# Graph kernel on one core: bias splits padded to 128 rows, one stacked matmul for four, and the end of a graph's preparation two units earlier

## What is computed

```python
# layer 0
adj0 = adj + eye; dis = adj0.sum(2) ** -0.5
x = layernorm(x + dis[:, :, None] * adj0 * dis[:, None, :] @ (x @ weight) + bias)
# layer 1
m_j = x @ W1[:D];  m_i = x @ W1[D:]
pre = m_j[:, None, :, :] + m_i[:, :, None, :] + b1          # one row per pair (i, j)
msg = gelu(layernorm(pre) * g1 + be1)
agg = einsum('bijo,bij->bio', msg, adj)                     # adj is about 6% full
out = layernorm(x + layernorm(concat([x, agg]) @ W2 + b2) * g2 + be2)
```

## Time and profile before

| | us |
|---|---|
| median of 3 runs | 4361.47 (4359.83 to 4365.68) |
| profiled execution | 4369.12 |
| its span | 4367.4 |
| PE busy, matmul | 4004.6 (92%) |
| ACT busy | 3479.5 (80%) |
| DVE busy | 3154.2 (72%) |
| POOL busy | 1499.9 (34%) |

### The profile page before, as it was taken

One profiled execution on the slowest core, in us unless ns is written; L12 is line 12 of the kernel. 1 busy time (PEld: TensorE's weight loads), 2 busy tenths in 40 slices (PEclk: granted clock), 3 DMA queues, 4 the chain that ended last, 5 costly groups with the idle time before them and its releaser, 6 DMA issues.

```text
span 4367.4 us, 95715 instructions
## 1 busy us (share of the span) xinstructions
PE 4004.6 (92%) x30270; PEld 3283.8 (75%) x30399; DVE 3154.2 (72%) x6981; ACT 3479.5 (80%) x9481; POOL 1499.9 (34%) x1205
## 2 busy tenths in 40 slices
PE   3799999999989999999999999999999999999998
PEld 2677777777768777778777777777777777777776
DVE  3577777777767777767777768777777777768776
ACT  2687888878868878877887878888888888878887
POOL 2333432233413334323343233343233343223331
PEclk8899999999989999999999999999999999999999
DMA  1222221122202222112221112222122221112210
GB/s 42 72 70 78 70 73 38 57 79 78 71 24 64 79 70 78 44 52 72 78 71 65 41 61 78 79 70 68 37 62 79 78 71 62 46 59 78 66 58 15
DMA packets 245645, 276.71 MB, mean 63 GB/s; under 512 B 22320, under 2 KB 204080, under 8 KB 245040
## 3 DMA queue, kind: packets, MB, share of 16 engines
q1 hardware_dynamic: 212272, 168.62, 12.9%
q0 software_dynamic: 32768, 100.70, 6.2%
HBM read 160.17 MB, written 109.05 MB: 62 GB/s over the span
## 4 chain that ended last, share of the span: by engine, by line
PE 56%; ACT 12%; issue 11%; POOL 9%; DVE 5%; DMA 4%; SPq 2%; POOLq 0%; DVEq 0%; ACTq 0%; PEldq 0%
PE z_even_ps L1264 11%; POOL table L449 9%; PE agg_odd_ps L1227 9%; PE z_odd_ps L1264 8%; PE agg_even_ps L1227 7%; ACT tmp L647 4%; PE z_even_ps L1260 3%; PE z_odd_ps L1260 2%; DMA nbr_heavy<-table 2%; PE p_ps L1146 2%; PE p_ps L1147 2%; PE p_ps L1090 2%; DMA table<-stage,row_id 2%; ACT msg L634 2%; ACT root L578 1%
## 5 line engine op out<-in xcount | busy, mean ns | idle before, releaser
L647 ACT ACTIVATE tmp<-nbr,r_sb 128x128 f32<-128x128 f32 x4864 | 1519.3, 389 | 29.1
L998 DVE SCALAR_TENSOR_TENSOR pick<-rank,root_p 128x512 f32<-128x512 bf16 (+3 forms) x1664 | 895.5, 566 | 69.8 <-ACT rank L597 69.8
L1028 DVE SCALAR_TENSOR_TENSOR spread<-rankT,nbr 128x512 f32<-128x512 bf16 (+3 forms) x1664 | 918.7, 580 | 0.0
L449 POOL DMA_INDIRECT table<-stage,row_id x512 | 617.9, 1207 | 551.5 <-issue 504.9
L1264 PEld LDWEIGHTS z_even_ps<-mi_g,pick 128*128 128x128 f32 x5120 | 643.9, 201 | 152.2 <-issue 152.2
L634 ACT ACTIVATE msg<-msg 128x768 f32<-128x768 f32 (+1 forms) x896 | 727.7, 812 | 32.3 <-issue 29.2
L1264 PE MATMUL z_even_ps<-mi_g,pick 128*128 128x129 f32 x5120 | 733.0, 295 | 0.0
L1264 PEld LDWEIGHTS z_odd_ps<-mi_g,pick 128*128 128x128 f32 x5120 | 608.8, 192 | 144.8 <-issue 144.8
L1264 PE MATMUL z_odd_ps<-mi_g,pick 128*128 128x129 f32 x5120 | 694.9, 285 | 0.0
L1227 PE MATMUL agg_odd_ps<-spread,msg 128*128 128x128 f32 x5120 | 671.8, 282 | 21.4 <-DVE spread L1028 19.3
L1227 PEld LDWEIGHTS agg_odd_ps<-spread,msg 128*128 128x128 f32 x5120 | 636.0, 199 | 24.1 <-DVE spread L1028 23.5
(11 more groups left out here) (206 smaller groups left out, 5129.6 us busy)
## 6 DMA issues: line engine op xcount, KB each, us to landing
nbr<-table SPq DMA_DIRECT2D x128, 512.0 KB, 4.0
adj_g<-in_adj SPq DMA_DIRECT2D x32, 1024.0 KB, 5.5
nbr_root<-table SPq DMA_DIRECT2D x128, 256.0 KB, 4.7
nbr_heavy<-table SPq DMA_DIRECT2D x512, 32.0 KB, 3.6
x_g<-in_x SPq DMA_DIRECT2D x32, 256.0 KB, 2.9
table<-stage,row_id POOLq DMA_INDIRECT x512, 2.7
out<-out_sb SPq DMA_DIRECT2D x32, 256.0 KB, 2.3
w_sb<-in_L_gnn_W SPq DMA_DIRECT2D x2, 128.0 KB, 2.3
```

Of the source, the lines that this page charges most:

```text
L449: pool.indirect_dma_start(table[q], bass.IndirectOffsetOnAxis(ap=row_id[:, jt * TB + it:jt * TB + it + 1], axis=0), stage[:, jt, it, :], N ...
L647: last = act.activation(tmp[:, c % 2, n - FROM[u], :], half_row, ACT.Identity, scale=r_sb[:, c % 2, n - FROM[u]:n - FROM[u] + 1])
L998: ins = dve.scalar_tensor_tensor(into.rearrange("p k n -> p (k n)"), rank[:, it, span], float(MARK + t), root_p[:, it, span], ALU.is_equal ...
L1028: ins = dve.scalar_tensor_tensor(into, rankT[:, it, jt:jt + count, :], float(MARK + t), nbr[:, it, jt:jt + count, 0:P], ALU.is_equal, ALU. ...
```

## The change

1. `be_split`, `mi_split` and `b2_split` have 128 partitions, zero from row 3 on, and the 3-row matrix of ones is replaced by the 128 x 128 one that exists already. The results are the same.
2. `T_HEAVY` is one matmul with 128 columns of weights in place of four with 32; for it DVE copies `edge_p[:, 0:32]` four times side by side (`edge_heavy`).
3. The norms go to four spare columns (400 to 403) of the bank `agg_odd_ps` with semaphores of their own, so they no longer take a place in the line for `p_ps` and stand in one step with the first `S_V`.
4. `S_Y`'s pair, `S_H`, `S_HT`, `S_MIT`, `S_MJT` and `S_NRM` stand one unit earlier, `S_V`, `S_MJ`, `S_MI`, `S_SEED`, `S_ROOT`, `S_OVER` and `S_SCATTER` two (the last read of `S_OVERS` one).

```diff
-S_Y, S_H, S_HT, S_MIT, S_MJT, S_NRM = 9, 12, 13, 14, 15, 16
-S_V = (17, 18, 19, 20)
-S_HB, S_MJ, S_MI, S_SEED, S_ROOT, S_SCATTER, S_OVER, S_OVERS = 18, 21, 22, 21, 23, 24, 23, 27
+S_Y, S_H, S_HT, S_MIT, S_MJT, S_NRM = 9, 11, 12, 13, 14, 15
+S_V = (15, 16, 17, 18)
+S_HB, S_MJ, S_MI, S_SEED, S_ROOT, S_SCATTER, S_OVER, S_OVERS = 18, 19, 20, 19, 21, 22, 21, 26
...
+NORM = 400
...
-        be_split = sb("be_split", [3, 3, D + 1], BF16)
-        ones3 = sb("ones3", [3, P], BF16)
+        be_split = sb("be_split", [P, 3, D + 1], BF16)
...
-                if s == S_Y + 1:
+                if s == S_Y:
                     wait_alone(pool, y_seq, a * POWS + 1)
...
                 if s == S_NRM:
-                    filled(F_NRM)
-                    act.activation(norm_j[:, :], p[:, 0:TB], ACT.Identity, scale=1.0 / D).then_inc(p_ev, 1)
-                    act.wait_ge(p_ev, a * NF + (F_NRM + 1))
+                    act.wait_ge(p_norm, a + 1)
+                    act.activation(norm_j[:, :], agg_ps[1][:, 0, NORM:NORM + TB], ACT.Identity, scale=1.0 / D).then_inc(p_normed, 1)
+                    act.wait_ge(p_normed, a + 1)
...
-                if (s, slot) == (S_Y + 2, 2):
+                if (s, slot) == (S_Y + 1, 2):
...
-                if (s, slot) == (S_PLACE, 0):
+                if (s, slot) == (S_POS, 4):
                     dve.wait_ge(p_fill, a * NF + (F_POS + 1))
...
+                if (t, slot) == (T_EDGE + 1, 2):
+                    dve.wait_ge(t_ev, n * NR + (R_EDGE + 1))
+                    dve.tensor_copy(edge_heavy[:, :, :], edge_p[:, 0:HEAVY_W].unsqueeze(1).to_broadcast([P, HEAVY_T, HEAVY_W])).then_inc(t_edge, 1)
...
                 if s == S_NRM:
-                    free(F_NRM)
+                    pe.wait_ge(p_ev, a * NF + (F_MJT + 1))
+                    if not is_int(a, 1):
+                        pe.wait_ge(p_normed, a)
                     for jt in range(TB):
-                        last = mm(p[:, jt:jt + 1], sqj[:, jt * P:(jt + 1) * P], ones[:, 0:1], start=True, stop=True)
-                    last.then_inc(p_fill, 1)
+                        last = mm(agg_ps[1][:, 0, NORM + jt:NORM + jt + 1], sqj[:, jt * P:(jt + 1) * P], ones[:, 0:1], start=True, stop=True)
+                    last.then_inc(p_norm, 1)
...
-                    for m in range(HEAVY_T):
-                        last = mm(p[m * HEAVY_W:(m + 1) * HEAVY_W, 0:P], edge_p[:, 0:HEAVY_W], lower[:, :], start=True, stop=True)
-                    last.then_inc(t_fill, 1)
+                    pe.wait_ge(t_edge, n + 1)
+                    mm(p[:, 0:P], edge_heavy[:, :, :].rearrange("p k w -> p (k w)"), lower[:, :], start=True, stop=True).then_inc(t_fill, 1)
...
-                        mm(z[:, h, :, :].rearrange("p k w -> p (k w)"), ones3[:, :], be_split[:, :, :].rearrange("p k w -> p (k w)"),
+                        mm(z[:, h, :, :].rearrange("p k w -> p (k w)"), ones_b[:, :], be_split[:, :, :].rearrange("p k w -> p (k w)"),
```

More of the change, by code:

```diff
@@ L55 @@
 S_X, S_SUP, S_PROD, S_PRE, S_CNT, S_CLS, S_POS, S_PLACE = 3, 5, 6, 8, 9, 10, 11, 12
-S_Y, S_H, S_HT, S_MIT, S_MJT, S_NRM = 9, 12, 13, 14, 15, 16
-S_V = (17, 18, 19, 20)
-S_HB, S_MJ, S_MI, S_SEED, S_ROOT, S_SCATTER, S_OVER, S_OVERS = 18, 21, 22, 21, 23, 24, 23, 27
[L60 to L63, removed]
+S_Y, S_H, S_HT, S_MIT, S_MJT, S_NRM = 9, 11, 12, 13, 14, 15
+S_V = (15, 16, 17, 18)
+S_HB, S_MJ, S_MI, S_SEED, S_ROOT, S_SCATTER, S_OVER, S_OVERS = 18, 19, 20, 19, 21, 22, 21, 26
+F_XT, F_AT, F_SUP, F_PROD, F_CNT, F_POS, F_HT, F_MIT, F_MJT, F_MJ, F_MI = (
+    0, 1, 5, 6, 7, 8, 9, 10, 11, 16, 17)
+F_V = (12, 13, 14, 15)
+F_OVER, NF = 18, 19
+NORM = 400
 SORT_FROM = 3
@@ L106, in adj_resnorm_kernel @@
         rest = sb("rest", [P, D])
-        b2_split = sb("b2_split", [3, D], BF16)
-        mi_split = sb("mi_split", [3, D], BF16)
-        be_split = sb("be_split", [3, 3, D + 1], BF16)
-        ones3 = sb("ones3", [3, P], BF16)
+        b2_split = sb("b2_split", [P, D], BF16)
+        mi_split = sb("mi_split", [P, D], BF16)
+        be_split = sb("be_split", [P, 3, D + 1], BF16)
         classes = sb("classes", [P, CLASSES])
@@ L171, in adj_resnorm_kernel @@
         edge_p = sb("edge_p", [P, N], BF16)
+        edge_heavy = sb("edge_heavy", [P, HEAVY_T, HEAVY_W], BF16)
         rank = sb("rank", [P, TB, N], BF16)
@@ L219, in adj_resnorm_kernel @@
         p_scat = [sem(f"p_scat{jt}") for jt in range(TB)]
-        p_seed, p_sq, p_new, p_cube, p_left = (sem(f"p_{n}") for n in ("seed", "sq", "new", "cube", "left"))
+        p_norm, p_normed, p_seed, p_sq, p_new, p_cube, p_left = (sem(f"p_{n}") for n in ("norm", "normed", "seed", "sq", "new", "cube", "left"))
         x_seq, y_seq, z_seq = sem("x_seq"), sem("y_seq"), sem("z_seq")
@@ L223, in adj_resnorm_kernel @@
         t_root = [sem(f"t_root{k}") for k in range(2)]
-        t_fill, t_ev, t_heavy, t_over = (sem(f"t_{n}") for n in ("fill", "ev", "heavy", "over"))
+        t_fill, t_ev, t_edge, t_heavy, t_over = (sem(f"t_{n}") for n in ("fill", "ev", "edge", "heavy", "over"))
         (c_pick, c_spread, c_zp, c_r, c_tmp, c_z, c_msg, c_agg) = (
@@ L723, in _ @@
             step(dve.tensor_tensor(b1_all, b1_all, g1_all, ALU.mult))
-            split(mi_split[:, :], b1_all)
-            split(b2_split[:, :], b2_all)
-            step(dve.memset(be_split[:, :, :], 0.0))
+            for rows in (mi_split[:, :], b2_split[:, :], be_split[:, :, :]):
+                step(dve.memset(rows, 0.0))
+            split(mi_split[0:3, :], b1_all)
+            split(b2_split[0:3, :], b2_all)
             for k in range(3):
-                split(be_split[:, k, 0:D], be1_all)
-            step(dve.memset(ones3[:, :], 1.0))
+                split(be_split[0:3, k, 0:D], be1_all)
             step(dve.memset(x_v[:, :], 1.0))
@@ L1129, in prepare @@
                         if s == S_MI:
-                            last = mm(dst, ones3[:, :], mi_split[:, :], start=False, stop=True)
+                            last = mm(dst, ones_b[:, :], mi_split[:, :], start=False, stop=True)
                     last.then_inc(p_fill, 1)
                 if s == S_NRM:
-                    free(F_NRM)
+                    pe.wait_ge(p_ev, a * NF + (F_MJT + 1))
+                    if not is_int(a, 1):
+                        pe.wait_ge(p_normed, a)
                     for jt in range(TB):
-                        last = mm(p[:, jt:jt + 1], sqj[:, jt * P:(jt + 1) * P], ones[:, 0:1], start=True, stop=True)
-                    last.then_inc(p_fill, 1)
+                        last = mm(agg_ps[1][:, 0, NORM + jt:NORM + jt + 1], sqj[:, jt * P:(jt + 1) * P], ones[:, 0:1], start=True, stop=True)
+                    last.then_inc(p_norm, 1)
                 if s == S_OVER:
@@ L1197, in overflow @@
                                 pe.wait_ge(o_sp, n + 1)
-                            mm(cols[:, :, 0:D + 1], ones3[:, :], be_split[:, 0:2, :], start=True, stop=False, skip_group_check=True)
+                            mm(cols[:, :, 0:D + 1], ones_b[:, :], be_split[:, 0:2, :], start=True, stop=False, skip_group_check=True)
                             for jt in (2 * k, 2 * k + 1):
@@ L1242, in steps @@
                     mm(u, aggT[:, k % 2, :], w2_sb[:, 1, :], start=False, stop=False)
-                    mm(u, ones3[:, :], b2_split[:, :], start=False, stop=True).then_inc(e_u, 1)
+                    mm(u, ones_b[:, :], b2_split[:, :], start=False, stop=True).then_inc(e_u, 1)
                 a, s = cx.prepared(i)
```

## The result

| | median us | lowest to highest | runs |
|---|---|---|---|
| kernel before | 4363.58 | 4359.83 to 4370.76 | 4 |
| changed kernel | 4059.80 | 4031.62 to 4082.12 | 4 |

The ratio is 0.9299 (95% interval 0.9239 to 0.9358): 304 us less, where 323 less was forecast, and 4059.8 where 4040 was. The profiled execution of the changed kernel took 4082.12 us with a span of 4080.3; against the 4369.12 of before that is 287 less. Its granted clock is 0.974 over the span.

The account below looks back on a forecast made before the run. ACT limits stage A (units 11 to 22), PE the other 16 units, stage B. 149 + 17 + 16 + 8 + 98 + 78 - 43 = 323 us less gives 4040 us, range 3930 to 4165.

Parts of the forecast that it names:

- padding in B: Bias groups of z in the 16 units limited by PE: 128 rows save 0.30 us a unit, 149 us.
- `b2_split`: Its bias groups for 2.3 tiles in the PE-limited stage: 128 rows save 0.24 us each, 17 us.
- A's yield: Units 11 to 22, limited by ACT: PE's savings mostly hidden, 0.5 us a graph counted, 16 us.
- the wait: PE's wait for tile 0's rows at L1159: transfers leave two units earlier, so it goes, 98 us.
- the low clock: Clock drop behind PE's wait at L1159: goes with the wait, 2.5 us a graph, 78 us.
- DVE's backlog: Unit of the wait at L1159: DVE work the wait hid costs back 1.4 us a graph, -43 us.
- a padded group keeps its cost: Rival at the bias groups: weight loads cannot run under matmuls of the same row group; 4214 us, chance 3%.
- A yields too: Rival in the ACT-limited stage: PE's 12 x 0.30 us count there, 112 us more, 3928 us; chance 11%.
- The low clock did not stay: Rival: the low clock stays or finds another place, as PE idles at ACT's root; 4118 us, chance 12%.
- ACT did not take B over: Rival in the PE-limited stage: ACT or DVE becomes its limit, gains there lost; 4214 us, chance 8%.
- Late all the same: Rival at tile 0's read: something else than the last indirect transfer holds SP; 133 us less gain, 4173, chance 3%.
- The slower outcome: Rival: PE idles behind the root in every graph and the clock stays at 1.2 GHz; 4702 us, chance 3%.

Follow-up runs that it names:

- 64-row kernel: The changed kernel with only the bias group ahead of z cut from 128 to 64 rows: 4204.7 us, ratio 0.9627 to the kernel before.
- semaphore kernel: The changed kernel with a semaphore for the 13th transfer, so SP's tile 0 read skips waiting for transfers 14 to 16: 4017.7 us, changed kernel 4078.9.
- 64- and 65-row kernels: The changed kernel with only the bias group ahead of z at 64 or 65 rows: 4204.7 us with 64, 4089.2 with 65.

## Right and wrong, point by point

The forecast of 323 us stands against 287 between the two profiled executions (and 304 between the medians):

| term | predicted | measured | from |
|---|---|---|---|
| padding in B | 149 | 149 | 0.30 us a unit, by starts and by the 64-row kernel |
| `b2_split` | 17 | 17 | units with it 0.54 shorter |
| A's yield | 16 | 0 | 50.85 to 50.90 |
| T_HEAVY | 8 | 8 | by starts, 0.16 to 0.056; not run alone |
| the wait | 98 | 41 | 97.7 to 56.4 |
| the low clock | 78 | 70 | 293.6 to 154.2 us at 1.2 GHz, half of the difference |
| DVE's backlog | -43 | about 0 | the rest |

The measured terms sum to 285 of 287. Part 1 and parts 3 and 4 were never run apart without the gaps above, so the split between them rests on the starts, the waits and the clock records, and for z's padding on the 64-row kernel.

That the total came so near is partly luck. For the wait, its clock and the backlog the prediction had 98 + 78 - 43 = 133, for a wait that goes; 41 + 70 = 111 came with half of the wait still there. With the wait gone, in the semaphore kernel, the same terms against the kernel before are 88 for the wait (97.7 to 10.0) and 108 for the clock (293.6 to 78 us at 1.2 GHz, half of the difference), less the 14 above: 182. With the 174 of the padding and T_HEAVY that is 356, and the spans differ by 355 (4367.4 and 4012.1). So the prediction was wrong that the wait goes and priced its going too low, and the two errors cancel in part.

- **Padding: right.** The way in, the group and the way out each lost what the rows of before said, 0.10 us. The rival by which a padded group keeps its cost (4214) falls. The Trainium skill's rule in TensorE: Matmul & The Clock Gate (What overlaps and what doesn't), that a load runs under a matmul only where the row group differs, is not borne out: z's first load stopped standing idle just when its rows became the same. The Trainium skill's TensorEngine Tiling (Key Properties) has a change of mode drain the engine; the 64- and 65-row kernels agree, with 0.10 in and 0.20 out at 64 and nothing at 65.
- **A: place right, yield wrong.** It begins at unit 9 and stays at 50.9; the 16 us did not come. The 64-row kernel shows more than I had seen: without the padding of z this stage would be 52.4 after the move. So moved work makes PE count in A, and the padding takes it back. The rival "A yields too" counted the 16 us of A twice: by its own terms it is 3944, not 3928.
- **The wait: wrong, the step that failed.** The prediction put it as "the transfers leave 2 x 4.7 us earlier against a wait of 2.9 us, so the wait goes", with POOL's 16 transfers back to back "in both". The lead was there, 9.9 us. That the 16 would take as long as before was not: they took 3.0 or 5.6 us more. "With nothing but their 0.30 us between" was read from one row; 16 equal issues of 0.96 us would take 18.9 us from first to last, and the kernel before already took 22.9. I also took the lead against the old start of unit 23, though my own part 1 brings that forward, by 3.6 us. And 9.4 of the 98 us lie ahead of the first unit, where the move changes nothing. With a semaphore of its own for the 13th transfer the wait within the graphs does go, to 3.8 us.
- **The clock: the number right, what stands for it too small.** Nearly the whole 78 came, though not all of the waits went; with the wait gone it is 108. Not all of the low clock stands behind that wait, as the prediction has it: some 31 us in one piece fall behind the extra matmuls of an overflow round at 1277 us (27 in the changed kernel), and 17 at the end of the run, and these stay. In the graph shown the clock stays at 1.00 behind 2.39 us of waiting, where it fell behind 2.94 in the graph of the earlier trace rows. No new wait at the root brought it down; PE's waits there grew a little but stay under 3 us each (for `mi_g` 30.1 us in all where it was 20.3, for `rankT` 26.9).
- **DVE's backlog: too large.** Where the wait is really gone, in the semaphore kernel, at most the 14 missing us can be it. I had 43 for waits twice as long in sum; per us of wait removed that is 0.30 against my 0.44.
- **Rivals.** The low clock did not stay (293.6 to 154.2 us), and A did not yield. ACT did not take B over (87% there). "Late all the same" came half true, but its mechanism, something else than the last transfer holding SP, is not what the trace shows. The slower outcome has no trace of itself.

**What makes an issue slow.** The traces narrow it down. DVE beside the transfer that starts at 1969.95 and ends at 1972.98, and the step with the same DVE work in the kernel before, where a transfer of 3.03 us starts at 2110.75 and ends at 2113.78:

```profile
1970.80 0.67 DVE L1032 SCALAR_TENSOR_TENSOR spread<-rankT,nbr 128x512 f32<-128x512 bf16 x1
1971.50 0.65 DVE L1032 SCALAR_TENSOR_TENSOR spread<-rankT,nbr 128x512 f32<-128x512 bf16 x1
1972.08 0.87 DVE L973 TENSOR_TENSOR msg<-z_odd_ps,tmp 128x384 f32<-128x384 f32 x2
```

```profile
2112.29 0.65 DVE L1028 SCALAR_TENSOR_TENSOR spread<-rankT,nbr 128x512 f32<-128x512 bf16 x1
```

Both issues end 0.83 us behind the end of a `spread`, when DVE has gone on to `msg`. Over the changed kernel 146 of the 147 issues of over 1.5 us end 0.83 us (to 0.03) behind a SCALAR_TENSOR_TENSOR of DVE that reads nothing from PSUM (`pick`, `spread`, `half`, `stage`), unlike `msg`, and from 0.13 us behind their start to 0.83 before their end such instructions cover 98% of the time. In the kernel before it is 66 of 70. So a slow issue lasts as long as a row of these instructions does, and the first two of them are DVE's ordinary work in every unit. Not each of them holds an issue: in 35 of the 189 that stay under 1 us one was running at that point too. No run leaves one out, so this is a reading of the traces and not an experiment.

## What to carry to other kernels

Give a small bias matmul as many rows as its neighbours have, or at least 65, if a row of zeros costs nothing: a 3-row group among 128-row groups cost 0.30 us each time, and 64 rows cost the same. When a producer is moved earlier to remove a wait, take the lead against the consumer's new place and the producer's duration in its new surroundings. And where a reader needs only part of a batch of transfers, give that part a semaphore of its own: it did here what the move alone could not, 61 us for a few lines.

## What was not expected

- POOL's issue of one indirect transfer took from 0.96 to 3.32 us in one graph; the same 512 took 540 to 745 us over the kernels run, and nearly every slow one ends 0.83 us behind one kind of DVE instruction.
- For whole sets of runs, every execution of the kernel before took 4.3 to 4.7% longer (4551.6 and 4571.8 against 4365), with PE supplied in drips while indirect transfers run. The changed kernel lost less to this (4119.5 against 4059.8 and 4078.9), so that the same change is worth a ratio of 0.901 or of 0.93. Kernels have to be compared inside one set.
- The step between 64 and 65 rows: 126 us of a 4 ms kernel hang on one row of zeros.
